# State-space attention: the own-token weight moves from products with the identity onto the diagonal of the attention weights

## The reference

```python
dt = softplus(dt + dt_bias);  v = x * dt[..., None];  D_res = x * D[None, None, :, None]
gc = cumsum(-exp(A_log) * dt, axis=1)
lam = softplus(L * dl)                       # one weight per level
decay = exp(where(causal, gc[t] - gc[s], -inf))
lam_ts = take_along_axis(lam, fenwick_level_map(T, NL))   # level 0 is the token itself
att = einsum('btgn,bsgn->bgts', Cm, Bm) * decay * lam_ts
y = einsum('bhts,bshp->bthp', att, v) + D_res
y = y * silu(z);  y = y * rsqrt(mean(y * y) + eps) * norm_w;  out = y @ out_proj_w.T
```

## Time and profile before

| | before |
|---|---|
| runs | 3472.71, 3478.15, 3478.8 us; median 3478.15 |
| profiled execution, its own time | 3471.38 us |
| its span from the first to the last instruction | 3469.6 us |
| mean granted TensorE clock | 0.914 |
| TensorE busy in the whole span | 83% |
| VectorE busy | 58% |
| ScalarE busy | 48% |
| GpSimd busy | 16% |

### The profile page before, as it was taken

One profiled execution on the slowest core, in us unless ns is written; L12 is line 12 of the kernel. 1 busy time (PEld: TensorE's weight loads), 2 busy tenths in 40 slices (PEclk: granted clock), 3 DMA queues, 4 the chain that ended last, 5 costly groups with the idle time before them and its releaser, 6 DMA issues. The chain is left out here.

```text
span 3469.6 us, 56019 instructions
## 1 busy us (share of the span) xinstructions
PE 2865.2 (83%) x19677; PEld 2097.6 (60%) x19677; DVE 2018.9 (58%) x5039; ACT 1665.8 (48%) x3702; POOL 543.2 (16%) x530
## 2 busy tenths in 40 slices
PE   6999999999879788488799764466998969996897
PEld 5777777777667567356566531355795545554685
DVE  6777787667569423688666668756012763334223
ACT  6666667666543222366576527233333335554221
POOL 2111011111122232100000000000110013333422
PEclk8999999999989799799899887667998989998898
DMA  3111111111100369200000000061994010001386
GB/s 128 46 38 37 38 46 38 37 38 38 37 23 2 145 210 302 72 2 2 24 11 8 29 0 0 0 103 68 342 344 137 1 53 26 26 26 65 131 275 205
DMA packets 143172, 273.47 MB, mean 79 GB/s; under 512 B 50576, under 2 KB 105104, under 8 KB 138032
## 3 DMA queue, kind: packets, MB, share of 16 engines
q1 hardware_dynamic: 126544, 237.60, 21.4%
q0 software_dynamic: 8688, 23.78, 1.8%
q10 hardware_dynamic: 7664, 8.51, 0.7%
HBM read 222.11 MB, written 47.74 MB: 78 GB/s over the span
## 5 line engine op out<-in xcount | busy, mean ns | idle before, releaser
L3008 ACT ACTIVATE L0a_ex<-bank,L0a_nb 128x128 f32<-128x128 f32 x512 | 145.2, 367 | 120.9 <-PE bank L2937 120.4
L1430 POOL TENSOR_TENSOR L3x_p<-L3x_p,L3x_rsum 128x512 f32<-128x512 f32 x128 | 130.6, 1040 | 415.5 <-DVE L3x_rsum L1501 415.5
L1483 DVE CUSTOM_DVE_ANT_0 L3x_s<-bank,L3x_bias 128x512 f32<-128x512 f32 x128 | 87.0, 681 | 177.7 <-PE bank L1259 177.7
L3274 DVE TENSOR_TENSOR L0a_ru<-bank,L0a_um 128x512 f32<-128x512 f32 x128 | 88.2, 689 | 170.8 <-PE bank L2929 156.3
L3265 DVE SCALAR_TENSOR_TENSOR L0a_xf<-L0a_xc,L0a_conv,L0a_xf 128x256 f32<-128x256 f32 x432 | 178.4, 480 | 9.3 <-ACT L0a_xf L3070 7.8
L3186 POOL TENSOR_TENSOR L0a_sum_sq<-L0a_sum_sq,L0a_sq 128x512 f32<-128x512 f32 x56 | 74.5, 1331 | 692.6 <-ACT L0a_sq L3105 692.6
L2851 PE MATMUL bank<-x_feat,L0a_wx 128*128 128x256 f32 x576 | 138.5, 392 | 4.1 <-ACT L0a_xc L3057 4.1
L2937 PE MATMUL bank<-L0a_ru,L0a_vm 128*128 128x512 f32 x256 | 134.2, 606 | 0.0
L2894 PE MATMUL bank<-x_feat,L0a_wz 128*128 128x256 f32 x512 | 119.5, 383 | 9.4 <-DVE L0a_yacc L3365 6.2
L1483 DVE CUSTOM_DVE_ANT_0 L1x_s<-bank,L1x_bias 128x256 f32<-128x256 f32 x256 | 92.9, 419 | 56.3 <-PE bank L1259 41.1
L2851 PEld LDWEIGHTS bank<-x_feat,L0a_wx 128*128 128x128 f32 x576 | 108.9, 195 | 25.4 <-issue 7.0
(11 more groups left out here) (707 smaller groups left out, 7514.2 us busy)
## 6 DMA issues: line engine op xcount, KB each, us to landing
L2f_wt<-in_L2f_w SPq DMA_DIRECT2D x23, 2180.0 KB, 9.2
L0f_wt<-in_L0f_w SPq DMA_DIRECT2D x39, 898.0 KB, 6.2
L3f_wt<-in_L3f_w SPq DMA_DIRECT2D x39, 768.0 KB, 5.5
L0a_wx<-in_L0a_wx SPq DMA_DIRECT2D x72, 256.0 KB, 3.1
L0a_wz<-in_L0a_wz SPq DMA_DIRECT2D x32, 512.0 KB, 4.3
L2a_band<-conv_taps SPq DMA_DIRECT2D x4, 2048.0 KB, 22.0
context_keys_values<-L2f_zeros ACTq DMA_DIRECT2D x32, 256.0 KB, 4.3
L0f_xs<-rows_by_expert SPq DMA_DIRECT2D x39, 128.5 KB, 3.3
```

Source lines behind the costliest of these rows:

```text
L1430: nc.gpsimd.tensor_tensor(p_, p_, rsum[g // n % 2][:, g % n, :].to_broadcast([P, NK]), ALU.mult).then_inc(sig("divided"), 1)
L1483: ins = vec.tensor_tensor_reduce(out=s[:, at:at + nk], in0=bank[:, at:at + nk], in1=bias[r % 2][:, e, :], scale=-scale, scalar=3e38, op0=A ...
L3008: last = a(ex[g % 3][:, j, b * P:(b + 1) * P], bank[:, at:at + P], ACT.Exp, bias=nb[r % 2][:, b, h:h + 1])
L3274: rv.empty(vec.tensor_tensor(ru[g % 2][:], bank[:].rearrange("p (j t) -> p j t", j=2), um[:].unsqueeze(1).to_broadcast([P, 2, T]), ALU.mult))
```

## The change

The identity products, the tile `xs` and VectorE's instruction that made it are gone. Instead GpSimd makes `own`, for every pair a 128 by 512 tile that is `coef` on the diagonal of each of the four 128 by 128 blocks and zero elsewhere (identity times `coef`, both read as broadcasts), one pair ahead and in two buffers. VectorE adds it to `ex` after the multiplication, with a wait between the two since they write the same tile. TensorE's `values` now waits for the sum.

```diff
-                    pe.wait_ge(sig("att"), g + 1)
-                    pe.wait_ge(sig("xs"), g // 2 + 1)
+                    pe.wait_ge(sig("weights"), g + 1)
 ...
                         for j in range(2):
-                            mm(y_bank[j * HD:(j + 1) * HD, ts], of(j, t), e[:, j, ts], start=True, stop=False)
-                        for j in range(2):
-                            own = g % 2 * P + j * HD
-                            last = mm(y_bank[j * HD:(j + 1) * HD, ts], xs[g // 2 % 2][:, t, own:own + HD], c.ident[:], start=False, stop=True)
+                            last = mm(y_bank[j * HD:(j + 1) * HD, ts], of(j, t), e[:, j, ts], start=True, stop=True)
 ...
+                def own_weights(g):
+                    r, i = divmod(g, NPH)
+                    if g == 0:
+                        pool.wait_ge(sig("misc"), index[("N", 3, KD - 1)] + 1)
+                    if i == 0:
+                        pool.wait_ge(sig("coef"), r + 1)
+                    if g >= 2:
+                        pool.wait_ge(sig("weights"), g - 1)
+                    by_pair = coef[r % 2][:].rearrange("p b h -> p h b")[:, 2 * i:2 * i + 2, :]
+                    tt(own[g % 2][:], c.ident[:].unsqueeze(1).unsqueeze(1).to_broadcast([P, 2, TB, P]),
+                       by_pair.unsqueeze(3).to_broadcast([P, 2, TB, P]), ALU.mult).then_inc(sig("own"), 1)
 ...
                 for s in steps:
+                    if 0 <= s + 1 < PAIRS:
+                        own_weights(s + 1)
 ...
-                    vec.tensor_tensor(by_head(xs[n % 2][:]), by_head(xt[r % 2][:, :, (p - 1) * T:p * T]),
-                       coef[r % 2][:, :, hs].unsqueeze(3).to_broadcast([P, TB, 4, HD]), ALU.mult).then_inc(sig("xs"), 1)
 ...
-                    vec.tensor_tensor(weights, weights, inner.unsqueeze(1).to_broadcast([P, 2, TB, P]), ALU.mult).then_inc(sig("att"), 1)
+                    ch.link(vec.tensor_tensor(weights, weights, inner.unsqueeze(1).to_broadcast([P, 2, TB, P]), ALU.mult))
+                    dve.wait_ge(sig("own"), g + 1)
+                    vec.tensor_tensor(weights, weights, own[g % 2][:], ALU.add).then_inc(sig("weights"), 1)
 ...
                 def direct(rho):
+                    if rho >= 2:
+                        dve.wait_ge(sig("own"), NPH * (rho - 1))
```

More of the change, by code:

```diff
@@ L2764, in layer0_attn @@
         ex = [sb(f"ex{i}", [P, 2, T]) for i in range(3)]
-        xs = [sb(f"xs{i}", [P, TB, T]) for i in range(2)]
+        own = [sb(f"own{i}", [P, 2, TB, P]) for i in range(2)]
         source_w, xw = [sb(f"source_w{i}", [P, H]) for i in range(2)], [sb(f"xw{i}", [P, T]) for i in range(2)]
@@ L2771, in layer0_attn @@
         stats, mv, rstd = sb("stats", [P, NT, 6]), sb("mv", [P, NT, 2]), sb("rstd", [P, NT, 3])
-        normed = lambda n, j: xs[j // 2][:, j % 2, :] if n == 3 else (yzT if n == 1 else zT)[:, j, :]
+        normed = lambda n, j: own[j // 2][:, j % 2].rearrange("p b t -> p (b t)") if n == 3 else (yzT if n == 1 else zT)[:, j, :]
         sig = Signals(nc, "L0a")
@@ L3236, in values @@
                     r, p = n // (NPH // 2), n % (NPH // 2) + 1
-                    if n == 0:
-                        turned_out(dve, ("N", 3, KD - 1))
                     taken(dve, ("XT", r, p))
-                    dve.wait_ge(sig("coef"), r + 1)
                     if n >= 2:
```

## The result

The changed kernel takes **3521.12 us** in the median of 4 runs (3514.59 to 3527.11), the kernel before 3475.61 beside it: a ratio of **1.013, 95% interval 1.0107 to 1.0154**. It is slower by 45 us; forecast was 3493, slower by 15, with 3512 as the upper end. The direction is right, the size is not, and the time lies outside the range.

What follows compares the result with a forecast made beforehand. The prediction took TensorE to bound steps 0 to 4, VectorE 4 to 8, both nearly full 8 to 12, and neither 12 to 0. A round +2.7 us, seven +19, last round -4: 3478 + 15 = 3493 us, range 3452 to 3512.

Steps and rivals of the forecast that it cites:

- 4 to 8: Steps 4 to 8 of a round, led by VectorE: additions and `own` collisions lengthen it by 3.5 us.
- 8 to 12: Steps 8 to 12 of a round, along VectorE: 3.5 us added, less its waits, makes +1.9 us.
- F of step 13: TensorE's item in step 13: 2.1 us late, from VectorE's 5.4 plus 0.12 less a 3.4 us distance after `xw`.
- the terms that I listed: Delays and savings behind F, steps 13 to 0: lateness grows from 2.1 to 4.5 us.
- the addition and its collision ahead of `far`: VectorE at step 13: 0.72 us for the addition plus 0.85 for meeting `own`, making `far` 3.7 us late.
- The last round: Round without convolution to collide with: TensorE saves up to 7 us, half counted, so -4 us.
- Step 0 to 4: Steps 0 to 4 of a round, TensorE alone: -1.8 us, the rest hidden by VectorE's idle 12 us.
- Short blocks: Rival: `own` holds VectorE up 0.2 us at most per collision, giving 3459 us; chance 0.22.
- TensorE alone: Rival: TensorE bounds everywhere and VectorE's additions hide, -56 us, giving 3422 us; chance 0.10.
- Longer blocks and a lower clock: Rival: `own` at 1.33 us blocks 0.25 more at eight places a round, TensorE's clock drops: 3512 us; chance 0.15.
- 12 to 0: Steps 12 to 0 of a round: VectorE begins 5.4 us late, 4.5 remain at the end; forecast -0.9 us.

Runs made afterwards that it cites:

- e1: The change with GpSimd building `own` only for the first two pairs, later additions using the old tiles: 3477.73 us, ratio 1.0011.
- e5: The change with TensorE's items of steps 7, 11 and 15 ordered E, F, Z, Z instead of F, E, Z, Z: 3519.99 us, ratio 1.0118.
- e10: The change with VectorE's `xw` and `far` ahead of `attend` and the addition: 3493.89 us, ratio 1.0048.
- b10: The kernel before with `xw` and `far` ahead of `attend`, and `xs` split off behind it: 3456.20 us, ratio 0.9945.
- e16: The change with products nobody reads put into TensorE's waits at step 13 and in the last round: 3521.38 us, ratio 1.0130.
- e3: The change without both `own` and the addition, own weights missing from the result: 3429.06 us, ratio 0.9866.
- e2: The change with `own` built but VectorE's addition left out, own weights missing from the result: 3450.83 us, ratio 0.9922.
- e15: The change without `own` and the addition, with `xw` and `far` first and chunk 7's first tap later: 3393.30 us, ratio 0.9753.
- b11: The kernel before with `xw` and `far` first, `xs` behind `attend`, and chunk 7's first tap behind step 13's exponents: 3436.42 us, again 3443.76.
- b8: The kernel before with ScalarE's first tap of chunk 7 moved behind the exponents of step 13: 3451.15 us, ratio 0.9932.
- e13: The change with `xw` and `far` first, `own` timed to VectorE's step start, and chunk 7's first tap later: 3442.99 us, ratio 0.9907.
- e14: b11 with VectorE itself adding own weights for pairs 12 to 15 and 0 to 3 of each round but the last: 3429.12 us, ratio 0.9871.
- b16: The kernel before with 10 products of no use in TensorE's wait at step 13: 3473.74 us, ratio 0.9993.

## Why the prediction was wrong in size

**Right.** Stretches 4 to 8 and 8 to 12 came out within 0.15 us, and by the mechanism named: GpSimd's `own` holds VectorE up, and the addition lengthens it by 0.72. The split is less exact than the sum. By e1, the addition and TensorE's saving make +0.41 from 4 to 8 where I had 1.12, and the collisions 3.10 where I had 2.35; two errors that cancelled, which is luck. Neither cost makes the loss alone: without `own` 10.7 of the layer's 45.8 us are left, without the addition the layer is 25.9 us shorter than before.

**The step that failed**, in the words of the prediction: "F of step 13 starts 3.4 us after `xw` has ended, so it is 5.4 + 0.12 - 3.4 = 2.1 late". This lets TensorE keep its old times while VectorE is late. Counted from step 4, F stood at 59.14 us before (501.52 in the earlier trace rows, less 442.38) and stands at 63.93 after (523.12 less 459.19): 4.8 late instead of 2.1. That is the whole error of the stretch; from F on, 2.4 were forecast and 2.45 measured. F did not wait for `xw`: it begins 2.55 us after `xw` has ended at 520.57. It is late because TensorE is: the turn of step 9 already begins 4.86 us late, and what four shorter values save from there to F goes into the waits around the two Z of step 11. Two lines earlier I had written that TensorE waits for VectorE from 8 to 12, and then forgot it. I had the Z's wait for `far` at step 7 and 15 only. Which wait carries it matters little: in e5 the second Z waits half as long, and F is still 4.4 late; in e10 the turn of step 9 has no wait for `far` any more, and is 4.4 us later than in b10, where VectorE's step 8 begins 4.9 earlier. TensorE follows VectorE by whatever wait is there.

The 2.45 behind F hold some clock as well. Of the change's stretch 1.2 us are the lower clock after the 5.25 us wait (e16), but the kernel before lost 0.77 in the same place in this round (32.11 against 31.34). So 0.4 of the 2.45 is the clock and 2.0 is left for the terms that I listed, against 2.4. The first of them, the addition and its collision ahead of `far`, is 1.44 (from F to the turn 8.12 us instead of 6.68), forecast 1.57. The others were not taken apart.

**The last round**, forecast -4: TensorE's saving came through there, all of it, when nothing else was added (e3: 83.10, -7.4), and my half of 7 for it was low. But I gave the addition no price in it. With it the round takes 94.84 even without collisions, 11.7 more, against 16 x 0.72 = 11.5 of added VectorE work; and the clock, 1.00 before and in e3, is 0.90 in e1. TensorE's 426 instructions take 70.34 us busy in e3 and 78.45 in the change. e16 won back 2.2 us of this with products in some of the waits. Its first twelve steps run at a clock of 1.00 and take 66.26 us, against 66.32 before and 61.09 in e3: with the clock out of it, the addition and the collisions take back there all that TensorE saves. How the loss of the last four steps (26.58, 24.14 before) divides between the addition and the clock stays open.

**Step 0 to 4** gained 1.29 instead of 1.8. Without the addition it is 26.78 (e2, e3), and with `xw` and `far` first as well (e10): 0.45 of the saving is lost to the addition in front of them.

**The rivals.** Short blocks is out: the collisions measure 35 us in the layer, 43 in the total. TensorE alone is out, though e15 shows what it would have been on a better order. Longer blocks and a lower clock came nearest, but not for its reasons: `own` takes 1.04 us alone and not 1.33, and the 0.7 us a round that it gave the clock is about what the clock takes (0.4 more than before in the fourth round). What it lacked is the lateness of TensorE, and any clock in the last round.

## What to carry to other kernels

When an engine becomes the late one, every engine that waits for it is late as well: a later chain must start from the waits of the new schedule, not from the old distance between two instructions. New work on a full engine should go behind whatever another engine wants in the same step; here that order was worth 27 us to the change and 21 to the old kernel, and with one more move (b11) 33 us of the old kernel's layer, nearly what the change could have saved there at most (39, e3). An edit that helps the change has to be tried on the kernel before as well, or it is taken for the cause. And where one stage of a long program is changed, its own time tells more than the total, which moves with the stages that nobody touched. Last, work saved on TensorE that turns into waits can cost again through the clock, so a stretch whose granted clock is below 1.00 is to be priced at both (33.25 and 29.43 us in e3).

## What the runs showed of the hardware

A VectorE instruction with two SBUF operands that meets a running two-operand GpSimd instruction is held until some 0.15 us before that one ends: `attend` lost 0.63 of the 0.76 us that `own` had to go, the residual addition 0.73 of 0.88. Operands read by broadcast make no difference that shows: beside `add_squares`, which has none, `xs` lost 1.07 of 1.21. The Trainium skill (SBUF — State Buffer, section on the two separate sides of SBUF) has the shared ports locked for the whole instruction. A full block of `own` would be 0.89 by these rows, an estimate (1.04 less 0.15), so between the 0.85 that I took and the 1.04 of that rule, and nearer to the first. It works both ways: the `own` of 465.23 took 1.69, while two VectorE instructions of that kind were running.

TensorE's granted clock need not be the same in rounds of the same work. In e3 the stretch 12 to 0 had 0.85 in two rounds and 1.00 in another, 33.25 and 29.43 us, with a wait of 3.80 us at step 13 in each. In b8, b11, e13, e14 and e15, where that wait is 0.8 to 2.0 us, and in e16 and b16, where products of no use fill it, the stretch had 1.00 in every round.
